# An attention and mixture-of-experts layer in fp32 on one core: expert groups taken two, two and one

## What is computed

```python
x = x + xattn(layernorm(x), ctx)            # 16 heads of 16, 77 keys per batch
h = layernorm(x)                            # N = 4096 rows
scores = softmax(h @ wg)                    # 8 experts
gates, idx = top_k(scores, 2)               # normalised to sum 1
# each (token, choice) gets a slot in its expert's list, at most C = 1280
disp = rows of h by slot                    # [8, 1280, 256]
y = silu(disp @ fc1_w.T + fc1_b) @ fc2_w + fc2_b      # hidden width 1024
res = h + gates[0] * y[slot 0] + gates[1] * y[slot 1]
out = x + layernorm(res) * gamma + beta
```

## Time and profile before

| | us |
|---|---|
| median of 3 runs | 799.65 |
| lowest, highest | 797.29, 800.08 |
| the profiled execution | 795.76 |
| its span | 794.0 |
| TensorE (PE) busy | 686.0 |
| VectorE (DVE) busy | 572.7 |
| POOL busy | 420.3 |
| ScalarE (ACT) busy | 395.4 |

### The profile page before, as it was taken

How to read it: one execution, slowest core, us unless ns; L and a number is a source line. 1 busy time by engine, 2 the same in 40 slices (tenths; PEclk the granted TensorE clock), 3 DMA queues, 4 the chain that set the end, 5 groups by cost and what they waited for, 6 DMA issues and landing times.

```text
span 794.0 us, 15751 instructions
## 1 busy us (share of the span) xinstructions
PE 686.0 (86%) x5636; PEld 651.8 (82%) x5636; DVE 572.7 (72%) x1232; ACT 395.4 (50%) x901; POOL 420.3 (53%) x470
## 2 busy tenths in 40 slices
PE   4899999999999723799999998999999999999400
PEld 3689999999989612699999998999999999999400
DVE  4699898988887778366566669878697566845078
ACT  2355555555555333345345457455474445634174
POOL 5845654654653202614644667868578554632466
PEclk9799999999999855699999999999999999999855
DMA  9400111101101120504524545445455342321374
GB/s 284 158 28 28 42 35 34 42 28 40 42 33 36 42 73 24 178 11 99 104 44 97 103 88 126 72 102 120 101 114 117 47 102 50 61 32 20 43 256 165
DMA packets 55332, 63.85 MB, mean 80 GB/s; under 512 B 9296, under 2 KB 50512, under 8 KB 55120
## 3 DMA queue, kind: packets, MB, share of 16 engines
q0 software_dynamic: 15360, 21.31, 16.6%
q1 hardware_dynamic: 34784, 40.96, 15.9%
q10 hardware_dynamic: 5104, 0.44, 0.4%
HBM read 38.96 MB, written 23.72 MB: 79 GB/s over the span
## 4 chain that ended last, share of the span: by engine, by line
PE 50%; issue 17%; POOL 15%; DVE 9%; DMA 6%; ACT 1%; SPq 0%; POOLq 0%; DVEq 0%; ACTq 0%
PE banks L750 15%; PE banks L752 15%; PE banks L751 15%; POOL xn L435 4%; POOL xn L438 4%; DMA sum_rows<-y_sb,slot_ids 4%; POOL X L431 2%; POOL rstd L486 2%; PE banks L970 2%; DVE oh_lo L1359 1%; DVE z L1470 1%; POOL rstd L411 1%; DMA wq_sb<-in_wqT 1%; DMA res<-sum_rows 1%; DMA xg<-xn_rows,slot_ids 1%
## 5 line engine op out<-in xcount | busy, mean ns | idle before, releaser
L520 POOL DMA_INDIRECT sum_rows<-y_sb,slot_ids x80 | 131.7, 1647 | 169.3 <-ACT y_sb L699 138.7
L709 ACT ACTIVATE hraw<-banks,b_now 128x256 f32<-128x256 f32 x320 | 132.4, 476 | 94.6 <-PE banks L752 83.8
L750 PE MATMUL banks<-xT_hi,w_hi 128*128 128x256 f32 x560 | 161.9, 289 | 0.0
L752 PE MATMUL banks<-xT_hi,w_lo 128*128 128x256 f32 x560 | 159.0, 284 | 0.0
L751 PE MATMUL banks<-xT_lo,w_hi 128*128 128x256 f32 x560 | 158.8, 284 | 0.0
L750 PE MATMUL banks<-w_hi,h_hi 128*128 128x256 f32 x528 | 148.9, 282 | 2.2 <-DVE y_sb L1402 1.1
L751 PE MATMUL banks<-w_lo,h_hi 128*128 128x256 f32 x528 | 148.6, 281 | 0.0
L752 PE MATMUL banks<-w_hi,h_lo 128*128 128x256 f32 x528 | 148.5, 281 | 0.0
L1416 DVE TENSOR_TENSOR h_lo<-hraw,h_hi 128x512 fp32r<-128x512 f32 x160 | 116.3, 727 | 5.5
L509 POOL DMA_INDIRECT xg<-xn_rows,slot_ids x80 | 90.7, 1134 | 54.3 <-DVE slot_ids L1375 34.7
L1414 DVE CAST h_hi<-hraw 128x512 fp32r<-128x512 f32 x160 | 76.7, 480 | 50.3 <-ACT hraw L709 49.1
(11 more groups left out here) (189 smaller groups left out, 1423.7 us busy)
## 6 DMA issues: line engine op xcount, KB each, us to landing
w1raw<-in_w1T SPq DMA_DIRECT2D x8, 1024.0 KB
w2raw<-in_w SPq DMA_DIRECT2D x8, 1024.0 KB
xn_rows<-xn SPq DMA_DIRECT2D x32, 128.0 KB, 1.7
sum_rows<-xn SPq DMA_DIRECT2D x32, 128.0 KB, 1.8
out<-z SPq DMA_DIRECT2D x16, 256.0 KB, 2.2
res<-sum_rows SPq DMA_DIRECT2D x7, 512.0 KB, 7.8
X<-in_x SPq DMA_DIRECT2D x2, 1280.0 KB, 13.5
xg<-xn_rows,slot_ids POOLq DMA_INDIRECT x80
```

Of the source, the lines that this page charges most:

```text
L520: g.indirect_dma_start(sum_rows, bass.IndirectOffsetOnAxis(ap=slot_ids[:, st, 1, q:q + 1], axis=0), y_sb[:, u, q, :], None, bounds_check=N ...
L709: a.activation(hraw[:, j // 2, j % 2, :], banks[:, j // 2, (j % 2) * 256:(j % 2 + 1) * 256], ACT.Silu, bias=b1_now[:, (c // SPE) % 2, j:j ...
L750: t_.matmul(o, a_hi, b_hi, start=first, stop=False)
L752: return t_.matmul(o, a_lo, b_hi, start=False, stop=last)
```

## The change

An expert's five groups are taken as three units: groups 0 and 1, groups 2 and 3, group 4. The first products of a unit of two have 512 columns, one block of hidden features per bank; group 4 has 256 as before, and so have groups 0 and 1 of expert 0. The banks of the first products become five (0, 1, 2, 3, 7) in turn, each freed by ScalarE's SiLU; `hraw` becomes a ring of three parts of 512 columns. The second products of a unit's tiles stand behind its first products: tiles 0 to 3 behind unit 0; after units 1 and 2 tiles 4 to 9. `xT` and `h` exist once, with three places of 256 columns, and no longer twice. `xg` is a ring of six groups and no longer of ten. TensorE reads `tokens_e` only for group 4 and tiles 8 and 9; groups 2 and 3 and tiles 0 to 7 are always multiplied. Some small buffers of the router move to a region that is reused.

```diff
-    XR = 2 * SPE
+    XR = SPE + 1
...
-        xT_hi, xT_lo = sb("xT_hi", [P, 2, DC, 2 * P], f32r, M), sb("xT_lo", [P, 2, DC, 2 * P], f32r, M)
-        hraw = sb("hraw", [P, 4, 2, 2 * P], f32, M)
-        h_hi, h_lo = sb("h_hi", [P, 2, HJ, 2 * P], f32r, M), sb("h_lo", [P, 2, HJ, 2 * P], f32r, M)
+        xT_hi, xT_lo = sb("xT_hi", [P, DC, 3 * 2 * P], f32r, M), sb("xT_lo", [P, DC, 3 * 2 * P], f32r, M)
+        HR = 3
+        hraw = sb("hraw", [P, HR, 512], f32, M)
+        h_hi, h_lo = sb("h_hi", [P, HJ, 3 * 2 * P], f32r, M), sb("h_lo", [P, HJ, 3 * 2 * P], f32r, M)
...
+        FC1_BANKS = (0, 1, 2, 3, 7)
+        TWO = slice(0, 2 * ST_ROWS)
+        FIRST, NEXT, LAST = (slice(n * ST_ROWS, (n + 1) * ST_ROWS) for n in range(3))
+        def chunks(e, unit):
+            if unit == 2:
+                return [((2 * k, 2 * k + 1), LAST) for k in range(HJ // 2)]
+            if e == 0 and unit == 0:
+                return [((2 * k, 2 * k + 1), cols) for cols in (FIRST, NEXT) for k in range(HJ // 2)]
+            return [((j,), TWO) for j in range(HJ)]
+        CPE = 2 * HJ + HJ // 2
+        def chunk_no(e, unit, k):
+            return CPE * e + HJ * unit + k
+        SILUS = [0]
+        for e_ in range(NE):
+            for unit_ in range(3):
+                for js_, cols_ in chunks(e_, unit_):
+                    SILUS.append(SILUS[-1] + len(js_))
...
+        def columns_of_group(st):
+            return (FIRST, NEXT, FIRST, NEXT, LAST)[st % SPE]
...
+            def silus(e, unit):
+                for k, (js, cols) in enumerate(chunks(e, unit)):
+                    c = chunk_no(e, unit, k)
+                    if e == 0 and unit == 0 and k == 2:
+                        rows_hi(1)
+                    wait(act, sem("h_lo_made"), c - HR + 1)
+                    act.wait_ge(sem("fc1_done"), c + 1)
+                    n = width(cols)
+                    for i, j in enumerate(js):
+                        a.activation(hraw[:, c % HR, i * n:(i + 1) * n], banks[:, FC1_BANKS[c % 5], i * n:(i + 1) * n],
+                                     ACT.Silu, bias=b1_now[:, e % 2, j:j + 1]).then_inc(sem("h_made"), 1)
...
+            for e in range(NE):
+                st = SPE * e
+                silus(e, 0)
+                rows_hi(st + 2)
+                rows_hi(st + 3)
+                scale_results(e, 0)
+                rows_hi(st + 4)
+                scale_results(e, 1)
+                next_quarter(e, 0)
+                scale_results(e, 2)
+                next_quarter(e, 1)
+                scale_results(e, 3)
+                silus(e, 1)
+                silus(e, 2)
+                rows_hi(st + SPE)
+                scale_results(e, 4)
+                if e + 1 < NE:
+                    scale_results(e, 5)
+                    rows_hi(st + SPE + 1)
+                    next_quarter(e, 2)
+                else:
+                    scale_results(e, 5)
+                scale_results(e, 6)
+                next_quarter(e, 3)
+                for tile in range(7, 10):
+                    scale_results(e, tile)
...
-                if before < FEW_FROM * ST_ROWS:
-                    products(True)
-                    return
...
+                    groups = (1 if e == 0 else 2, 4, 5)[unit]
+                    pe.wait_ge(sem("xT_hi_made"), SPE * e + groups)
+                    pe.wait_ge(sem("xT_lo_made"), SPE * e + groups)
+                    for k, (js, cols) in enumerate(chunks(e, unit)):
+                        c, n = chunk_no(e, unit, k), width(cols)
+                        if e == 0 and unit == 0 and k == 2:
+                            transpose_rows(1)
+                        if cols == NEXT and k == HJ // 2:
+                            pe.wait_ge(sem("xT_hi_made"), 2)
+                            pe.wait_ge(sem("xT_lo_made"), 2)
+                        if c >= 5:
+                            pe.wait_ge(sem("h_made"), SILUS[c - 4])
+                        for i, j in enumerate(js):
+                            hs, o = slice(j * P, (j + 1) * P), banks[:, FC1_BANKS[c % 5], i * n:(i + 1) * n]
+                            if used:
+                                for k_ in range(DC):
+                                    m = mm3(o, w1_hi[:, w, k_, hs], w1_lo[:, w, k_, hs], xT_hi[:, k_, cols],
+                                            xT_lo[:, k_, cols], k_ == 0, k_ == DC - 1)
+                            else:
+                                m = t_.matmul(o, w1_hi[:, w, 0, hs], xT_hi[:, 0, cols], start=True, stop=True)
+                        m.then_inc(sem("fc1_done"), 1)
+                if unit == 2:
+                    if_tokens(e, 4 * ST_ROWS, columns)
+                else:
+                    columns(True)
...
+                wait(pe, sem("y_made"), t - 1)
...
+                        for k, (js, cols) in enumerate(chunks(e, unit)):
+                            if j == js[0] and cols.start <= rows.start < cols.stop:
+                                pe.wait_ge(sem("h_lo_made"), chunk_no(e, unit, k) + 1)
+                        m = mm3(o, h_hi[:, j, rows], h_lo[:, j, rows],
+                                w2_hi[:, w, j, :], w2_lo[:, w, j, :], j == 0, j == HJ - 1)
...
+            for e in range(NE):
+                st = SPE * e
+                fc1(e, 0)
+                transpose_rows(st + 2)
+                fc2(e, 0)
+                transpose_rows(st + 3)
+                fc2(e, 1)
+                transpose_rows(st + 4)
+                fc2(e, 2)
+                fc2(e, 3)
+                fc1(e, 1)
+                fc1(e, 2)
+                transpose_rows(st + SPE)
+                fc2(e, 4)
+                fc2(e, 5)
+                transpose_rows(st + SPE + 1)
+                fc2(e, 6)
+                fc2(e, 7)
+                def last_two(second_used):
+                    if second_used:
+                        fc2(e, 8)
                     else:
+                        if_tokens(e, 4 * ST_ROWS, lambda used: fc2(e, 8, used))
+                    fc2(e, 9, second_used)
+                if_tokens(e, 4 * ST_ROWS + P, last_two)
...
+            def biased(e, tile):
+                st, q = SPE * e + tile // 2, tile % 2
+                if q == 0:
+                    wait(dve, scattered[st % 2], 32 * (st // 2))
+                dve.wait_ge(sem("fc2_done"), 2 * st + q + 1)
+                v.tensor_tensor(y_sb[:, st % 2, q, :], banks[:, YB + q, 0:D], b2_sb[:, e, :], ALU.add)\
+                    .then_inc(sem("y_made"), 1)
+            def hidden(e, unit):
+                read = 2 * SPE * e + (-2, 4, 0)[unit]
+                for k, (js, cols) in enumerate(chunks(e, unit)):
+                    c, j = chunk_no(e, unit, k), js[0]
+                    if e == 0 and unit == 0 and k == 2:
+                        rows_lo(1)
+                    if k == 0:
+                        wait(dve, sem("fc2_done"), read)
+                    raw = hraw[:, c % HR, :].rearrange("p (j t) -> p j t", j=len(js))
+                    hi, lo = h_hi[:, j:j + len(js), cols], h_lo[:, j:j + len(js), cols]
+                    dve.wait_ge(sem("h_made"), SILUS[c + 1])
+                    v.tensor_copy(hi, raw).then_inc(sem("h_hi_made"), 1)
+                    dve.wait_ge(sem("h_hi_made"), c + 1)
+                    v.tensor_tensor(lo, raw, hi.bitcast(f32), ALU.subtract).then_inc(sem("h_lo_made"), 1)
...
+            for e in range(NE):
+                st = SPE * e
+                hidden(e, 0)
+                rows_lo(st + 2)
+                biased(e, 0)
+                rows_lo(st + 3)
+                biased(e, 1)
+                rows_lo(st + 4)
+                next_quarter_lo(e, 0)
+                biased(e, 2)
+                next_quarter_lo(e, 1)
+                biased(e, 3)
+                hidden(e, 1)
+                hidden(e, 2)
+                rows_lo(st + SPE)
+                biased(e, 4)
+                biased(e, 5)
+                rows_lo(st + SPE + 1)
+                next_quarter_lo(e, 2)
+                biased(e, 6)
+                next_quarter_lo(e, 3)
+                for tile in range(7, 10):
+                    biased(e, tile)
```

More of the change, by code:

```diff
@@ L259, in attention_steps, with width @@
             step(PAIRS + 1, 0)
-        def expert_steps(engine, step):
-            for c in range(NST + 3):
-                step(0, c)
+        ST_ROWS = 2 * P
+        FC1_BANKS = (0, 1, 2, 3, 7)
[15 more added lines that the diff above has]
+                    SILUS.append(SILUS[-1] + len(js_))
+        def width(cols):
+            return cols.stop - cols.start
+        def columns_of_group(st):
+            return (FIRST, NEXT, FIRST, NEXT, LAST)[st % SPE]
         def res_loaded(engine, t):
@@ L1423, in expert_step, with next_quarter_lo @@
+            def next_quarter_lo(e, n):
+                if within(e + 1, NE):
+                    par = (e + 1) % 2
+                    wait(dve, sem("fc2_done"), 2 * SPE * e)
+                    dve.wait_ge(sem("w_hi_made"), 4 * (e + 1) + n + 1)
```

(1 more changed line is left out.)

181 lines of the change are left out of this document (47 added, 134 removed).

## The result

| | before | after |
|---|---|---|
| median, us | 799.04 (4 runs) | 851.32 (4 runs) |
| lowest, highest | 797.29, 800.08 | 849.71, 856.96 |
| the profiled execution | 795.76 | 856.96 |
| its span | 794.0 | 855.2 |

The ratio is 1.067, 95% interval 1.062 to 1.072: slower by 52 us, where 18.5 were forecast and the range ended at 832. The sign was right, the size was not.

What follows compares the result with a forecast made beforehand. TensorE was taken to bound the expert part. Work 419.8 plus waits 20.2 less the present 417.3 gave +22.7; start -1.7 and end -2.5 made +18.5 us, so 818 on the median of 799.65; range 808 to 824, outer 798 to 832.

Steps and rivals of the forecast that it cites:

- stops at tile 0 behind short experts: TensorE waiting for the hidden layer at the next expert's tile 0: 2.0 us behind experts 2, 3, 4, 6 (fifth group empty).
- placeholders (tile 7's bias, readings): Ends of experts 2, 3, 4, 6: tile 9's placeholder waits 1.5 us for tile 7's bias; token-count readings cost 0.5.
- lower rows: Ends of experts 2, 3, 4, 6: TensorE's transposes wait 0.4 us for VectorE's lower rows of the next expert's first group.
- the end: After the last product: scalings follow at once, last landing 7.7 us after it in place of 10.2, -2.5 us.
- the start: Expert part's first products no longer wait for the second group's gather: begin at 323.6 in place of 325.29, -1.7 us.
- I take the middle, 20.1: Short experts' group 2 scatter: landing 4.0, 6.2 or 7.6 us after its second half starts at 13.9; middle taken, 20.1.
- the third rival: VectorE or POOL becomes the bound: every landing at 7.6, VectorE stretched 0.1 us per part; 828 us, chance 0.17.
- I cost this at nothing: VectorE and POOL sharing more in dense stretches: nothing in the sum, up to +8 us in the range.
- a stop costs its own length: TensorE's waits entered as their durations; half clock counted only at the expert part's beginning, 2.4 us.
- Three slots of the hidden ring and five banks let TensorE run on: Next expert's first products: TensorE runs through all eight parts while VectorE is late, so the debt shows only at tile 0.
- 225 ns: Cost of each 512-column first product on TensorE, 213.3 + 11.7; 720 of them 162.0 us, the width giving back 8.6.
- does not grow: Part of a product's time beside its columns, taken as 11.7 ns at 512 columns too; if it doubles, 237 ns.

Runs made afterwards that it cites:

- load-later run: Kernel after, with SP's second weight load (`w2raw`) held until tiles 0 to 3 of the next expert are multiplied: 820.9 us, ratio 1.029.
- the two largest: Two edits of the kernel after: POOL's scatter issued ahead of the gather, 808.2 us; gathers issued three groups ahead in place of four, 811.8 us.
- scatter-first run with conditional tiles: Kernel after with POOL's scatter ahead of the gather, and tiles 6 and 7 multiplied only where they hold tokens: 818.6 us, ratio 1.027.

## Why the prediction was right and wrong

The terms of the expert part, as I put them and as the trace of after has them:

| us | forecast | measured |
|---|---|---|
| work without the width | 257.8 | 257.8 |
| 720 products of 512 columns | 162.0 | 167.4 (x 0.2325) |
| stops at tile 0 behind short experts, for a bank too | 9.6 | 26.3 |
| placeholders (tile 7's bias, readings) | 8.0 | 6.4 |
| lower rows | 1.6 | 4.3 |
| other stops | 1.0 | 4.6 |
| products at half clock behind the stops | 0 | 9.8 |
| sum | 440.0 | 476.6, of 479.0 |

Some 2.4 us are in gaps too small to count. (Measured stops are the gaps between starts beyond the pace; 103 products at half clock cost 0.095 each.)

**Right.** The work, instruction for instruction; the place: the end of short experts, through the bias of tile 8, though not behind expert 6; the gather that stands ahead of the scatter; the end (6.9 us after the last product, forecast 7.7); the start (relative to the lists 1.1 us earlier, forecast 1.7).

**Wrong: "I take the middle, 20.1".** Counted from the end of unit 1 of expert 2 (490.66), the scatter's second half starts at 15.6 (forecast 13.9) and lands at 23.5 (forecast 20.1). Half of these 3.4 us is the landing, 7.92 and not 6.2. The cause was on the record twice: the third rival says that the weight loads are issued just when group 2 is scattered, and the earlier trace rows has the 7.6. A middle between two states is wrong when the order of the program always picks one; the second load's place on SP should have been followed to its time, and it is issued 0.1 to 0.2 us after that scatter in experts 0 to 5, which land in 7.2 to 8.2 us, and not at all in expert 6, which lands in 3.8. The load-later run shows it: 3.8 to 5.1 us. The other half of the 3.4 us is the later start: tile 5 was scaled at 9.7, forecast 8.95, and the gather was issued 0.9 us after that.

**Wrong: "I cost this at nothing".** VectorE's eighth part was forecast 9.25 us after ScalarE's first; it took 527.79 - 516.11 = 11.7, since 1.15 us per part became 1.49 beside POOL's additions of `beta` (1.12 without them). With the scatters late, POOL's queue is full just when VectorE must catch up. TensorE makes a part in 6 x 0.2325 = 1.40, so VectorE makes up nothing. The term was bounded by +8 over all experts; the run without `beta` gives 25. The Trainium skill (SBUF — State Buffer, "SBUF: two separate sides") has a port pair that VectorE and GpSimd share, locked by whichever comes first for its whole instruction. The casts of 1.08 and subtractions of 1.14 us beside additions of 1.30 agree with it in direction. I had carried it only to the scatter's issue, not to VectorE's own passes.

**Wrong: a stop costs its own length.** Behind every group of stops at tile 0 the granted clock falls (to 0.83 in the 20 us around at three places and 0.91 at two) and 10 to 20 products cost 0.095 more each. In the earlier trace rows a stretch with 2.97 us of stops had kept 1.00, and from that I took nothing for it; the stops at tile 0 are several, with three products between, and 4 us long. The sum lacks 9.8 us for it.

**Wrong: "Three slots of the hidden ring and five banks let TensorE run on".** They let it run through five parts; in four experts the sixth waited for a bank 1.2 to 1.8 us. So a late landing is paid twice, at the bank and at tile 0.

**Wrong by 5.4: 225 ns.** The part beside the columns is 0.2325 - 0.2133 = 19 ns, between "does not grow" and "doubles" (11.7 and 23.7). By this pace the width's worth is 720 x 0.0045 = 3.2 us, not 8.6; the expert parts of one pair of profiles gave 2.3.

**And other places:** I had 2.0 us behind experts 2, 3, 4 and 6 and 0.8 behind 1 and 5. Expert 1 and expert 5, with one empty tile, stop at the next tile 0 for 3.8 to 4.1 us as well as 2, 3 and 4 do, and expert 6 not at all. Behind expert 6 both the load and the additions of `beta` are missing, so this place alone doesn't say which of them spares it. All these errors are in one chain, and a debt there is passed on whole, since VectorE needs at least as long per part as TensorE. Rival 3 named this chain, and its 828 was too low, since it had neither the half clock nor VectorE's full stretch. The second part of the cause is that the cover was gone: before, a hidden layer of the next group stood in front of the waiting biases; now it stands behind them.

What stays open: how the 52 us divide between the collision, the order and POOL's sharing. Each edit alone removes 25 to 43 us, and the two largest take away the delay and the collision at once, so the shares do not add up, and only their common origin, the gather's wait for its ring, is shown (40 us by the gathers three groups ahead).

## What to carry to other kernels

A ring made smaller is a new wait: write down on which queue it stands and which instruction is issued behind it, then follow that one to every transfer that it now meets. When a landing takes 4 or 8 us depending on what runs beside it, find out which case the order picks, and don't take the mean. An engine that needs as long per step as the one it feeds makes up no delay at all, and products of empty tiles can be the cheapest cover there is.

## What the runs showed of the hardware

- The indirect scatter with addition of group 2 landed in 3.8 to 5.1 us alone (load-later run), and in 7.2 to 8.2 where a 1 MB load was issued 0.1 to 0.2 us after it (after, experts 0 to 5).
- fp32 products of 512 columns start 0.2325 us apart, 19 ns beside their columns, against 11.8 ns at 256.
- Four stops of 0.7 to 1.1 us, with three products between them, put TensorE at the lower clock level for 10 to 20 products; in the scatter-first run with conditional tiles stops of 6.3 us in one stretch brought it to 0.83 there.
- Beside an fp32 addition of 1.30 us on POOL, casts of 0.42 us on VectorE took 1.08 and subtractions of 0.69 took 1.14. With gathers and scatters alone on POOL casts took at most 0.69 and subtractions 0.77.
